# The pixel loads of a vision-transformer kernel are issued from ScalarE's queue instead of SyncE's

## What is computed

```python
shifts = [(1, -1, 0, 0), (-1, 1, 0, 0), (0, 0, 1, -1), (0, 0, -1, 1)]
xs = jnp.concatenate([x] + [_shift(x, s) for s in shifts], axis=1)
t = xs.reshape(B, C5, h, 16, w, 16).transpose(0, 2, 4, 3, 5, 1).reshape(B, h * w, 3840)
mu, var = jnp.mean(t, -1, keepdims=True), jnp.var(t, -1, keepdims=True)
h = jnp.einsum('bnp,pd->bnd', (t - mu) * rsqrt(var + EPS) * ln_gamma + ln_beta, W) + b
h = concatenate([cls_tok, h]); h = h + attention(layernorm(h)); h = h + experts(layernorm(h))
```

## Time and profile before

| | before |
|---|---|
| median of 3 runs | 155.68 us |
| profiled execution, whole time | 155.41 us |
| its span, first to last instruction | 153.5 us |
| PE busy | 134.4 us (88% of the span) |
| ACT busy | 91.0 us (59%) |
| DVE busy | 108.5 us (71%) |
| DMA queue of SP (q1) | 9,562 packets, 17.25 MB |
| DMA queue of ACT (q10) | 360 packets, 0.34 MB |

### The profile page before, as it was taken

How to read it: one execution, slowest core, us unless ns; L and a number is a source line. 1 busy time by engine, 2 the same in 40 slices (tenths; PEclk the granted TensorE clock), 3 DMA queues, 4 the chain that set the end, 5 groups by cost and what they waited for, 6 DMA issues and landing times.

```text
span 153.5 us, 4141 instructions
## 1 busy us (share of the span) xinstructions
PE 134.4 (88%) x1630; PEld 105.3 (69%) x1630; DVE 108.5 (71%) x280; ACT 91.0 (59%) x219; POOL 50.6 (33%) x63
## 2 busy tenths in 40 slices
PE   0239999999999989995679999998899999999991
PEld 0115887794478878984458868886587778787881
DVE  6389959989896999547475999857947623723753
ACT  0398695975997674683279868555544444444430
POOL 7000000500001432000005324586568386477430
PEclk9999999999999999999999999999999999999999
DMA  4999992780002323004995000485000000000003
GB/s 121 398 337 393 286 301 57 241 320 8 0 0 59 71 71 67 4 0 117 394 395 228 0 4 6 112 317 208 0 0 4 0 2 0 4 0 2 0 4 119
DMA packets 9941, 17.85 MB, mean 116 GB/s; under 512 B 2758, under 2 KB 6162, under 8 KB 9922
## 3 DMA queue, kind: packets, MB, share of 16 engines
q1 hardware_dynamic: 9562, 17.25, 34.0%
q10 hardware_dynamic: 360, 0.34, 0.8%
HBM read 16.63 MB, written 0.96 MB: 115 GB/s over the span
## 4 chain that ended last, share of the span: by engine, by line
PE 68%; DVE 10%; ACT 8%; issue 6%; ACTq 3%; POOL 2%; DVEq 0%; POOLq 0%
PE PS L684 20%; PE PS L714 10%; PE PS L458 4%; PE PS L408 3%; PE PS L495 3%; PE PS L573 3%; PE PS L542 3%; PE PS L431 2%; PE PS L429 2%; PE PS L432 2%; POOL vhl L1061 2%; DVE vhl L1448 2%; PE PS L556 2%; PE PS L395 2%; PE PS L599 2%
## 5 line engine op out<-in xcount | busy, mean ns | idle before, releaser
L1070 POOL TENSOR_TENSOR kq<-vhl,kq 128x296 f16<-128x296 f32 x35 | 28.7, 821 | 43.5 <-ACT kq L987 43.5
L1448 DVE SCALAR_TENSOR_TENSOR vhl<-PS,vhl 128x296 f32<-128x296 f32 x36 | 16.8, 465 | 19.9 <-POOL vhl L1061 10.5
L980 ACT ACTIVATE vhl<-PS 128x296 f32<-128x296 f32 x36 | 14.9, 415 | 24.3 <-PE PS L684 22.9
L987 ACT ACTIVATE kq<-vhl 128x296 f16<-128x296 f32 x36 | 16.0, 446 | 6.6 <-DVE vhl L1448 6.4
L1061 POOL TENSOR_TENSOR vhl<-vhl,xs 128x296 f32<-128x296 f32 x14 | 12.6, 899 | 5.6 <-issue 4.9
L1046 POOL TENSOR_TENSOR piece<-stage,piece 128x768 f16<-128x768 f32 (+1 forms) x3 | 4.6, 1525 | 22.7 <-DVE mx L1315 22.7
L1437 DVE TENSOR_TENSOR vhl<-vhl,xs 64x296 f32<-64x296 f32 (+1 forms) x18 | 10.2, 566 | 2.6 <-ACT vhl L980 2.4
L684 PE MATMUL PS<-XAh,piece 128*128 128x296 f16 x48 | 9.5, 290 | 1.6 <-ACT XAh L865 0.7
L684 PE MATMUL PS<-XAh,slab 128*128 128x296 f16 x48 | 10.0, 291 | 0.9 <-DVE vhl L1448 0.9
L431 PE MATMUL PS<-whl,xhl 128*128 128x193 f16 (+1 forms) x40 | 10.5, 263 | 0.0
L429 PE MATMUL PS<-whl,xhl 128*128 128x193 f16 (+1 forms) x40 | 10.5, 263 | 0.0
(11 more groups left out here) (233 smaller groups left out, 375.9 us busy)
## 6 DMA issues: line engine op xcount, KB each, us to landing
slab<-in_w_inner_dram SPq DMA_DIRECT2D x3, 960.0 KB, 9.5
xs<-gate_rows_dram SPq DMA_DIRECT2D x8, 296.0 KB, 5.7
xs<-in_x_inner_dram SPq DMA_DIRECT2D x3, 592.0 KB, 10.5
stage<-in_f_a_dram SPq DMA_DIRECT2D x2, 768.0 KB, 4.9
stage<-in_f_b_dram SPq DMA_DIRECT2D x2, 768.0 KB, 6.8
stage<-in_f_d_dram SPq DMA_DIRECT2D x2, 576.0 KB, 8.2
xhl<-in_f_a_dram SPq DMA_DIRECT2D x1, 768.0 KB, 9.3
xhl<-in_f_b_dram SPq DMA_DIRECT2D x1, 768.0 KB, 10.6
```

What stands on the lines that cost most here:

```text
L980: A(silu[:, i % 2, :], PS[:, 3 + 2 * (i % 2), 0:HALF], ACT.Silu, scale=1.0 / XW).then_inc(S["a_silu"], 1)
L987: A(ah[:, f % ABUF, half * HALF:(half + 1) * HALF], hf[:, i % 3, :], ACT.Copy).then_inc(S["a_ah"], 1)
L1070: G.tensor_tensor(al[:, f % ABUF, cols], hf[:, i % 3, :], ah[:, f % ABUF, cols], ALU.subtract).then_inc(S["g_al"], 1)
L1448: V.scalar_tensor_tensor(out=hf[:, i % 3, :], in0=PS[:, 4 + 2 * (i % 2), 0:HALF], scalar=SH / XW, in1=src[:, i % 2, :], op0=ALU.mult, op1= ...
```

## The change

The function that loads a round of pixels moves from SyncE's program to ScalarE's. SyncE issues `gbs` and the four weight loads one after another, and then what it issued before. ScalarE issues the constants, the four pixel loads, and then its 13 small loads. The bytes, the buffers, the semaphores and all compute are the same.

```diff
@@ SyncE
-            def load_pixels(i):
-                rows, src = (P, x_inner[:, 2 * i:2 * i + 2, :]) if i < 3 else (RK, x_ring)
-                sp.dma_start(xsv[0:rows, 2 * i:2 * i + 2, :], src).then_inc(d_x[i], 16)
-
             for i in range(4):
                 load_weights(i)
-                load_pixels(i)
@@ ScalarE
+            def load_pixels(i):
+                rows, src = (P, x_inner[:, 2 * i:2 * i + 2, :]) if i < 3 else (RK, x_ring)
+                nc.scalar.dma_start(xsv[0:rows, 2 * i:2 * i + 2, :], src).then_inc(d_x[i], 16)
+
             nc.scalar.dma_start(cst[:, :], consts).then_inc(d_cst, 16)
+            for i in range(4):
+                load_pixels(i)
             nc.scalar.dma_start(tokb[0:1, :], tok_b).then_inc(d_rows, 16)
```

## The result

| | before | after |
|---|---|---|
| median (lowest to highest) | 155.47 us (154.63 to 157.39) | 159.58 us (158.87 to 160.02) |
| profiled execution, its span | 155.41, 153.5 us | 158.87, 157.0 us |
| PE busy | 134.4 us | 133.6 us |

Four runs of each. The changed kernel takes 1.0279 times as long, with a 95% interval of 1.0214 to 1.0344: slower. The two profiled executions stand 3.5 us apart.

The account below looks back on a forecast made before the run. ScalarE's issuing was taken to bound the kernel up to 11 us, TensorE from 13.4 to 32.2. Round 0's weights, landing at 10.3, shift the first compute: 155.41 + 2.5, other terms 0, gives 157.9 us; range 156.0 to 160.2.

Parts of the forecast that it names:

- signs of being wrong: Round 0 weights landing after 10.9 or before 9.8, a pixel issue over 1 us, or first patches other than 4.3 us.
- strict alternation: Rival at round 0's weight landing: engines take nothing in ahead, all pixels pass first; 12.1, +4.3 us, 159.7 us; chance 0.20.
- F: Start of `first_shift(0)`, ScalarE's first compute: 7.82 us before, forecast 10.3, +2.5 us; later work keeps its distances behind it.
- ScalarE's issues, 0.5 us each: Four more issues ahead of ScalarE's first compute, 2.0 us together, making it ready at 9.8 us.
- The weights of round 0 at 10.3: Landing on SyncE's queue: 20 of 30 pixel packets per engine pass first, 3.7 us on top of 6.6.
- some 28 of the 40 weight packets are ahead: Per engine, before round 1's pixels arrive; only the last 12 weight packets then alternate with further pixels.
- bundles of 13: Rival on queue turns: some 13 packets per turn, 4.4 us of pixels first; weights at 11.0, +3.2 us, 158.6 us; chance 0.10.
- Is the shift passed on?: Patch stage: round 1 weights at about 15.5, 1.2 us late but covered; TensorE still sets the stage's end.
- the 0.8 us that I left VectorE at the norm: VectorE's remaining slack at the end of the patch stage: 0.45 + 1.6 - 1.2 us.
- The vanished waits are worth nothing: ScalarE's waits for `awst` (1.69 us) and `stage` (1.60) vanish but are off the path; counted 0.
- TensorE's rate, 0 within -1.4 and +1.5: Round 0 patches: earlier rate doubling saves 1.4 us, doubling only at their end loses 1.5; taken as 0.
- the forecast's own: Narrower range of the main forecast, without its rivals: 157.0 to 158.9 us.

Follow-up runs that it names:

- e2: Changed kernel, with ScalarE issuing the four pixel loads behind all its small loads: 160.45 us, ratio 1.031 to the kernel before.
- e9: Kernel before, all patch loads still on SyncE's queue, but the four pixel loads ahead of the four weight loads: 162.82 us, ratio 1.0415.
- e1: Changed kernel, with the eight small loads of `tabs` and `jrev` issued by SyncE behind the attention weights: 160.16 us, ratio 1.0265 to the kernel before.
- e10: Kernel before, plus four loads of one 768-byte row each into an unused tile, issued by ScalarE behind the constants: 156.62 us, ratio 1.0064.
- e3: Kernel before, with only the pixel load of round 0 moved to ScalarE's queue, behind the constants: 156.13 us, ratio 1.0042.
- e4: Kernel before, with the pixel loads of rounds 0 and 1 moved to ScalarE's queue: 158.16 us, ratio 1.0139.
- e5: Changed kernel, each pixel load issued as two, with packets of 2,368 instead of 4,736 bytes: 160.02 us, one run.
- e6: Kernel before, plus 16 unused matmuls on a tile of ones ahead of TensorE's first beta rows and 8 behind: 157.57 us, ratio 1.0085.
- e7: Changed kernel, plus 38 unused matmuls on a tile of ones ahead of the first beta rows and 8 behind: 162.04 us, ratio 1.0384.

## Why the prediction was right or wrong

The time, 159.58 us, lies within 156.0 to 160.2, but not where I put it: I forecast 157.9 and within 2%, and it came out slower by 2.8%. All three of my signs of being wrong are there: the weights of round 0 landed after 10.9, a pixel issue took over 1 us (1.10), and the first patches took 3.60 instead of 4.3. What comes nearest is the rival "strict alternation" (159.7 us, 0.20): its landing of 12.1 is the measured one. Its premise holds only in part, as the engines did take some weights ahead.

**Where the kernel is bound, and the carrying number F.** Right. Patches behind F by 5.5 to 5.6 us hold in all kernels but e2, and span follows F down to e9's 7.3 us.

**ScalarE's issues, 0.5 us each.** Three took 0.5, the fourth 1.10; ready at 10.35 instead of 9.8. It did not matter, as it then waited 1.74 us. e1 shows that. Smaller issues can be cheaper: those of one row in e10 cost 0.35, that of one pixel load in e3 0.45.

**The weights of round 0 at 10.3.** This is the step that failed. "By then some 28 of the 40 weight packets are ahead" was taken from `cls`, which found the engines filled with weight packets and nothing else. In the changed kernel the pixels are issued at the same moment as the weights, and both queues fill the engines. When the first pixel packet starts, at 3.68 us, 89 weight packets have started, under 6 on each engine and not 28. The weights run ahead once more near 6 us (75 packets against 24 from 6.0 to 6.4), where the pixels of round 0 end, and from 7 us on the queues move 318 against 315.

How many pixel packets passed ahead of the last weights? 460 of 480, so 29 on each engine instead of 20. Priced as I did, 5.5 x 460 / 480 = 5.3 us instead of 3.7: 11.9 us, and 12.0 was measured.

My sum had a second gap, which it did not name: it treats the 16 engines as one. Counted over all of them, the 640th weight packet had started by 9.9 us with 23 pixel packets on each engine, near my 10.3. The last engine was 2 us behind that, in a stretch in which all engines together slowed from 412 GB/s (9 to 10 us) to 347 and 218 (10 to 12 us). Why they are not level, and why they slow down, no run shows. In e9, with one queue, the lag is there too: 1,105 weight packets had started when the first 640 had landed.

Rows that I had could have warned: the earlier trace rows were the only ones in which both queues held work from the same moment, and they showed one for one; the earlier trace rows showed a queue that came later. I used the second for a case of the first kind.

The size of a turn is one packet from 7 us on, by the stretches of 0.24 us above. By the Trainium skill, "DMA: Bandwidth & Descriptors", section "Queues, rings and completion order", a turn is typically 9 to 17 descriptors. The trace of this case does not agree: from 7 us on the two queues alternate row by row. For bundles of 13 I had worked the landing out as 11.0 us, and 12.0 was measured. The landing alone would not settle it, as my 24 pixel packets were too few: three full turns of 13 hold all 30 of an engine, and give 12.1 too. How much the engines take in ahead is not a fixed number of packets (`cls` in e9 against before, 8 packets against 28), but what bounds it no run separates.

**Is the shift passed on?** Right in direction, too small in size. The weights of round 1 came at 17.5, not 15.5, and ScalarE waited 1.61 for them, not about 1. TensorE was covered as I said, just: VectorE's operand for round 1 was ready at 22.10 + 0.55 = 22.65 and TensorE came to those patches at 23.29, 0.6 us later where it had been 2.5. Of the 0.8 us that I left VectorE at the norm nothing remains. By these 0.6 us and VectorE's end at 35.77, weights of round 1 that come still later should set the end of the stage instead of TensorE; no run shows it.

**The vanished waits are worth nothing.** Right. ScalarE has no wait for `awst` or `stage` any more, and from the norm to the end nothing is gained (121.2 us in both).

**TensorE's rate, 0 within -1.4 and +1.5.** It was -0.73 (3.60 against 4.33 us for the patches of round 0). The idle time ahead of the squares, forecast 1.3, is 15.47 - 14.27 = 1.2 us. In e3, e4, e5 and e9 the same patches take 4.5 to 4.7 us, in e2 4.1 and in e10 3.2, and F does not order these. I had no ground for a sign here, and still have none.

**The sum, redone:** F +4.27, patches of round 0 -0.73, nothing behind: +3.5 us, and the spans differ by 3.5. Between the medians lie 4.1 us, which the ratio's interval (3.3 to 5.3 us) holds together with 3.5.

That strict alternation's 159.7 is so close to 159.58 owes something to luck, as does that my range holds the time at all (the forecast's own went to 158.9). Of strict alternation, F was right to 0.03 us, but it had counted 0.7 us too much for TensorE, and the median of the runs lies 0.7 us above the profiled execution.

## What to carry to other kernels

In these runs a load that was moved to a second DMA queue competed with the first by packets, not by need: the queue with the large rows got most of the bandwidth, and the small rows, for which everything waited, came late. Order within one queue was the only priority that these runs had: first what is wanted first. So ask of a split what lies ahead of the load that starts the chain, once with both queues filled from the same moment; and read how two queues share from a stretch in which both started together.

## What the runs showed of the hardware that was not expected

- Two queues that are both filled moved equal numbers of packets in spite of their sizes: 145 to 144 with 1,536 and 4,736 bytes, 223 to 221 with 1,536 and 2,368. In the changed kernel they alternate packet by packet, 16 to 16 in each 0.24 us from 7.00 on.
- A DMA lands when its slowest engine is through, and that can be long after the mean: in the changed kernel 641 weight packets had started by 9.9 us, and the landing of the first 640 came at 12.0.
- A late-coming load waits for what the engines have taken in of the other queue: `cls`, issued at 1.74, starts at 4.92 in the kernel before, behind some 28 packets on each engine, and at 4.46 in e9, behind 8 larger ones.
- A DMA issue costs its engine 0.35 us for one row when nothing holds it up (e10) and 7.03 us when it is held up behind other loads (SyncE's `wring`, above).
- A later start of the patches can be free: in e10 1.1 us of delay came back whole, as the patches of round 0 then took 3.23 us instead of 4.33.
- TensorE can run at 1.2 GHz for several microseconds amid dense work (e10 from 73 to 80 us, granted clock 0.50 to 0.53, 1.0 us of span), and what brings it about is open. A difference of 1% between two kernels is worth a look at the granted clock by stretches before it is explained by anything else.
- The landing of the last result took 3.4 us in e10 instead of 1.9, which is more of its span than the clock.
- VectorE's small instructions on 37 partitions take 2.6 to 3.2 times as long (e6: 1.50 against 0.57 us for four; e7: 1.44 against 0.45 for two) while a GpSimd memset lies over them.
